# A message stream in DRAM with rows of 576 bytes in place of 516, in a two-layer graph network on one core

## What is computed

```python
h = jnp.maximum(_layernorm(x), 0.0)
# layer 0: mean over the neighbours, two products, log_softmax
agg = segment_sum(h[src], dst) / maximum(counts, 1)[:, None]
x = x + log_softmax(agg @ W_l.T + h @ W_r.T + b)
h = jnp.maximum(_layernorm(x), 0.0)
# layer 1: a weight for every edge, and a sum by the edge's source
weight = maximum(edge_attr @ W1 + b1, 0) @ W2 + b2
msg = (h @ Wl + bl)[dst] * weight
out = x + segment_sum(msg, src)
```

## Time and profile before

| | |
|---|---|
| median of 3 runs | 4677.88 us |
| the profiled execution, its own time | 4644.02 us |
| its span, first to last instruction | 4642.2 us |
| mean granted TensorE clock | 0.815 |
| busy: TensorE, VectorE, ScalarE, GpSimd | 78%, 57%, 39%, 37% |
| bytes by DMA | 468.65 MB, 101 GB/s over the span |

### The profile page before, as it was taken

One profiled execution on the slowest core, in us unless ns is written; L12 is line 12 of the kernel. 1 busy time (PEld: TensorE's weight loads), 2 busy tenths in 40 slices (PEclk: granted clock), 3 DMA queues, 4 the chain that ended last, 5 costly groups with the idle time before them and its releaser, 6 DMA issues.

```text
span 4642.2 us, 96340 instructions
## 1 busy us (share of the span) xinstructions
PE 3605.8 (78%) x24907; PEld 2626.4 (57%) x24908; DVE 2637.6 (57%) x7188; ACT 1823.9 (39%) x3754; POOL 1740.7 (37%) x1753
## 2 busy tenths in 40 slices
PE   2999999989877777777677677777777677778887
PEld 1666666657554455445455455555555445457776
DVE  7888888876444444444444444444444444457776
ACT  4666666643222222222222222222222222258887
POOL 2100000001255555555555555555555555520000
PEclk9999999995577777777777777777777777789999
DMA  3599600000023223332233333333332332258787
GB/s 90 183 318 316 212 5 6 6 1 10 23 78 76 77 76 76 78 76 77 76 76 77 76 77 76 77 77 75 78 76 77 77 76 76 76 150 223 224 225 211
DMA packets 572233, 468.65 MB, mean 101 GB/s; under 512 B 289293, under 2 KB 543334, under 8 KB 572181
## 3 DMA queue, kind: packets, MB, share of 16 engines
q1 hardware_dynamic: 515782, 348.95, 29.1%
q0 software_dynamic: 56400, 119.07, 7.5%
HBM read 235.79 MB, written 231.94 MB: 101 GB/s over the span
## 4 chain that ended last, share of the span: by engine, by line
PE 36%; another core or an unknown queue 27%; issue 18%; DVE 10%; ACT 5%; DVEq 2%; ACTq 1%; DMA 0%; POOL 0%; POOLq 0%; SPq 0%
PE PS L980 10%; PE PS L1092 5%; PE PS L1104 4%; PE PS L971 4%; DVE X L904 3%; PE PS L1081 3%; PE PS L1140 3%; DVE aux L659 2%; ACT big L1281 2%; PE PS L1073 1%; PE PS L1089 1%; ACT big L1269 1%; DVE H L893 1%; DVEq L899 1%
## 5 line engine op out<-in xcount | busy, mean ns | idle before, releaser
L492 POOL DMA_INDIRECT messages<-big,idxr x1664 | 1619.1, 973 | 1313.8 <-DVE big L865 811.4
L1104 PE MATMUL PS<-par,big 128*128 x4992 | 598.0, 268 | 753.1 <-ACT big L1281 706.7
L865 DVE TENSOR_TENSOR big<-PS,big 128x512 f32<-128x512 f32 x416 | 287.8, 692 | 1502.3 <-ACT big L1281 1142.5
L1104 PEld LDWEIGHTS PS<-par,big 128*128 128x128 bf16 x4992 | 479.6, 114 | 881.8 <-issue 805.4
L1281 ACT ACTIVATE big<-PS 128x512 f32<-128x512 f32 x416 | 248.4, 597 | 1325.3 <-remote 1121.3
L980 PE MATMUL PS<-par,aux 128*128 128x386 bf16 x3626 | 683.3, 327 | 0.0
L1092 PE MATMUL PS<-W2s,big 128*128 128x128 f32 x3328 | 678.1, 367 | 0.0
L1092 PEld LDWEIGHTS PS<-W2s,big 128*128 128x128 f32 x3328 | 576.6, 261 | 145.9 <-issue 145.9
L1202 ACT ACTIVATE aux<-PS 128x784 bf16<-128x784 f32 x592 | 479.7, 822 | 295.2 <-PE PS L971 288.2
L1269 ACT ACTIVATE big<-PS,b1c 128x512 f32<-128x512 f32 x416 | 284.4, 684 | 647.1 <-issue 424.5
L1140 PE MATMUL PS<-big,H 128*128 128x128 f32 x3456 | 444.0, 281 | 80.4 <-DVE H L893 64.1
(11 more groups left out here) (202 smaller groups left out, 3761.3 us busy)
## 6 DMA issues: line engine op xcount, KB each, us to landing
messages<-zeros SPq DMA_DIRECT2D x576, 193.5 KB
big<-messages SPq DMA_DIRECT2D x216, 516.0 KB, 3.7
aux<-slot_rows SPq DMA_DIRECT2D x416, 128.0 KB
big<-in_edge_attr_dram SPq DMA_DIRECT2D x1664, 32.0 KB
messages<-big,idxr POOLq DMA_INDIRECT x1664
X<-in_x_dram SPq DMA_DIRECT2D x6, 448.0 KB, 11.9
out_dram<-X SPq DMA_DIRECT2D x6, 448.0 KB
edge_places<-big SPq DMA_DIRECT2D x1, 2496.0 KB, 13.1
```

Of the source, the lines that this page charges most:

```text
L492: pool.indirect_dma_start(strm_d, bass.IndirectOffsetOnAxis(ap=idxr[:, n % U, j:j + 1], axis=0), outr[:, n % U, j, :], None).then_inc(S_sc ...
L1104: last = nc.tensor.matmul(pHG[:, j * C:(j + 1) * C], oht[:, k % 2, j * P:(j + 1) * P], h1p[:, ds(at + a * C, C)], start=(a == 0), stop=(a ...
```

## The change

A row of the stream gets 144 words (576 bytes) in place of 129 (516 bytes). Words 0 to 127 are the message, word 128 is the node's number, as before; the 15 words behind it are padding. The DMAs move whole rows, so the scatter, the filling with zeros and the loads of the last stage all move the padding too. The row of zeros is 2 rows long in place of 3, so the filling takes 864 DMAs of 147,456 bytes in place of 576 of 198,144. The padding in `outr` is never written by the computation, so one memset on VectorE clears the tile before the first message. ScalarE's bias takes the one column that it needs.

```diff
@@ -54,7 +54,7 @@
-    ROW = C + 1
+    ROW = C + 16
@@ -151,7 +151,7 @@
-        ZW = 3 * ROW
+        ZW = 2 * ROW
@@ -822,6 +822,7 @@
             dve.wait_ge(S["z_done"], NCH)
+            nc.vector.memset(outr, 0.0)
             nc.vector.memset(hotW, 0.0)
@@ -1302,7 +1303,7 @@
-                    last = nc.scalar.activation(away[:, t, :], iotaF[:, :], ACT.Abs, bias=fin[:, k, r, q * ROW + C:(q + 1) * ROW])
+                    last = nc.scalar.activation(away[:, t, :], iotaF[:, :], ACT.Abs, bias=fin[:, k, r, q * ROW + C:q * ROW + C + 1])
```

## The result

The changed kernel takes **4688.73 us** (median of 8 runs, 4681.45 to 4692.62), the kernel before 4678.56 in the same comparison (8 runs, 4672.25 to 4680.43). The ratio is 1.0024 [1.0015, 1.0032]: 10.2 us slower, just past the 0.2% that I said can be told. The time is 8.4 us above the forecast and inside its range. It also lies inside the 4671 to 4690 that I gave to the likeliest case, no change, but the interval of the ratio, 7 to 15 us slower, says that no change is not what came.

What follows compares the result with a forecast made beforehand. TensorE bounds layer 0, no engine is full while messages are made, VectorE's chain bounds the sums. Terms 2.4 + 0 + 0 + 0 on 4644.02 us give 4646.4; with 33.86 to the median, 4680.3 us, range 4658 to 4704.

Steps and rivals of the forecast that it cites:

- the likeliest case: Whole kernel: the forecast of 4680.3 us holds, too near the old time to tell apart, within 4671 to 4690; chance 69%.
- Zeros: Filling in layer 0: 0.55 us a DMA, 864 DMAs, done at 647 to 721 us, wanted at 1021; cost 0.
- Scatters: GpSimd's 1664 indirect DMAs while messages are made: 973 ns each as before; cost 0, with 2 us as the bound.
- The rival in which GpSimd becomes the pace: Messages: dearer scatters pace the steps, 920 us slower, or 188 us in a milder form; together 6%.
- The memset: VectorE's clearing of 2304 words ahead of the first messages: 1.9 to 2.5 us, taken as 2.4, nothing hiding it.
- a shifted rhythm: Messages: the later start shifts the pattern of steps, up to 20 us either way; 4% faster, 6% slower.
- The loads of the last stage: While messages are summed: 2.0 us on each engine, under the piece's 2.35; landings about 0.1 us later; cost 0.
- the odd piece: Last stage: an allowance of 3 us for occasional pieces delayed by a later landing, beside a cost taken as 0.
- the tight piece: Last stage: the one piece shown, ScalarE done 0.10 us before VectorE; if all 216 were so, at most 28 us; 6%.
- the sign of being wrong: Message steps shorter or longer than 6.9 us on average, or TensorE waiting for ScalarE's one-hot matrices (L1310) in the last stage.
- Faster by part-written pieces of 64 bytes: Messages: rows of 576 bytes avoid part-written pieces that hold steps back; 749 us less, a tenth being 75; 9%.
- The rule against the change: DMA reads split at 256 bytes, so whole 64-byte pieces earn nothing; a pair of rows some 4% dearer; sum unchanged.

Runs made afterwards that it cites:

- the one with the padding memset: The change with its memset on the 240 words of padding alone in place of all 2304, against the kernel before: 4652.15 us, ratio 1.0013.

## Why the prediction came out as it did

- **Zeros: right in the cost of nothing, a little dear in the size.** Forecast 0.55 us a DMA, filling done 647 to 721 us; measured 0.510 and 615, under the range. The line through 60 and 72 ns put a row of reads and a row of writes together, and the 72 has the queue's other small transfers in it; by its own working the new DMA takes 290 x 16 x 0.848 / 579 / 16 = 0.42 us on each engine for my 0.50. The cover of 300 us or more was there, and nothing moved.
- **Scatters: right.** 973 ns as before, 144 steps for 145, in traces of different clocks. The rival in which GpSimd becomes the pace did not come, nor any part of it.
- **The memset: the size right, what stood behind it left out.** 1.98 + 0.55 us for 2.4. "I take 2.4 us" was the account's whole sum for the entry. The first chip's traces put the entry at some 4 us: behind the memset TensorE does its first products at the granted clock of 0.50 where it had 1.00, and the first messages fall together in other pairs. I had named a shifted rhythm as a rival, with 6% on the slow side; the shift at the start came in every kernel with the full memset, but as a rhythm that holds on it is not shown: on the first chip the messages take as long as before. With the memset alone the median rose by 8.1 us, with an interval from 0.9 to 9.8.
- **The loads of the last stage: the step that failed.** "Landings come 0 to 0.23 us later, about 0.1 ... I take 0, and 3 us for the odd piece." I let the landing follow the engine's work, and the work was well forecast (2.05 us for 2.0). But a load lands with the last of its 16 parts, and with rows of 576 bytes the last few fall behind: 4.2 to 4.5 us in place of 3.7. I read the tight piece rightly, 0.10 us to spare; what I lacked was a landing later than my upper bound. The cost measured is 6.4 and 4.3 us in the change's two traces, and 3.0 in the one with the padding memset. What I had named as the sign of being wrong, TensorE waiting for L1310, is there with 8.0 us. That the late landings make the cost is shown from two sides: it goes with the length that lands late (572 and 580 bytes land at 3.9 and 4.0 and lose 1.0 and 1.2 us in the stage), and with eight buffers it is gone, though loads land as late. Why they land late is open.
- **Faster by part-written pieces of 64 bytes: half true and worth nothing.** The engines do have less work for the zeros of the new rows than for those of 572 bytes. The queue in 250 to 540 us, the change first and then 572 bytes:

```profile
q1 hardware_dynamic: 83280, 85.32, 84.8%
```

```profile
q1 hardware_dynamic: 79270, 80.64, 96.2%
```

290 x 16 x 0.848 / 83280 is 47.2 ns a transfer, and 290 x 16 x 0.962 / 79270 is 56.3, for zeros of 1152 and 1144 bytes (nine in ten of the queue's transfers are zeros, the rest are smaller). By the same working 1088 and 1280 bytes, whole pieces of 64 too, take 45.1 and 52.1, and 1160, which aren't, 52.5. But the 1548 bytes of the kernel before, which aren't either, take 63.9, no more a byte than the whole ones (0.041 ns). So not every transfer with a part-written piece pays alike. In the middle stage queue 1 stands at 16.5% for 19.5% in 2000 to 3000 us, with nearly the same packets. But the filling has 400 us to spare, and in the middle stage no engine waits for a DMA: the steps stayed what they were.
- **The rule against the change** (the Trainium skill, DMA: Bandwidth & Descriptors, How a descriptor splits into AXI transactions) has reads split at 256 bytes, so that whole pieces of 64 gain nothing. For reads the last stage decides nothing: 300 x 16 x 0.861 / 66518 = 62.1 ns a transfer in the change, and by the same working 62.3 at 572 bytes, no gain; but 64.1 at 580, and at 544, whole pieces again, 58.2, as little as at 516 (58.0). What it says of reads alone can't speak for the writes of the zeros, and they do gain: 47.2 for 56.3 ns. Late parts of a load follow from neither. The nearest thing in the Trainium skill (DMA: Bandwidth & Descriptors, Latency and other measured facts) is that a row pitch of large powers of two in device memory slows copies, which it puts down, as an inference, to memory channels hit in lock step; no run here reaches those pitches, and whether rows of 576 and 640 bytes meet something of the kind was not tried.
- **The sum.** Forecast +2.4, measured +10.2 and +8.4: the last stage's part is 4 to 6, the entry's some 4. Both terms erred to the same side. The range held because the odd piece and the shifted rhythm were in it; my 69% for no change leaned on a last-stage cost of zero that had a tenth of a microsecond of cover in the one piece that I read. That the time lies even inside the 69% case's 4671 to 4690 is luck: its mechanism, a last stage that loses nothing, did not hold.

## What to carry to other kernels

Where consumers take loads with little to spare, ask when the slowest of a load's 16 parts lands, not what a load costs on average: the new rows cost the engines 2.05 us a load, as forecast, and yet the loads landed later than their work says. More buffers, with the loop unrolled to match, took that cost away with its cause unknown, and paid with the old rows too (7.3 and 7.1 us). An instruction for which TensorE has to wait is to be priced with what follows it: here one of 2.5 us with its gap cost some 4, with TensorE's clock granted at the full level later behind it. And a difference of a few microseconds wants the chip on which the runs lie closest, 5.7 us against 17.9 and 18.6 here.

## What the runs showed that I had not expected

- The same kernel takes 4646.03, 4671.83 and 4675.78 us on three chips, 0.6% apart, while its 33 runs on the first span 5.7 us (4642.58 to 4648.31) and those on the others three times as much. The difference lies while messages are made: the kernel with eight buffers and rows of 516 bytes has 4103.2 - 1244.7 = 2858.5 us from first to last message on the first chip and 4131.9 - 1246.3 = 2885.6 on the third, while its last stage takes 500.6 and 501.2. The granted clock from 1270 to 4100 us is 0.73 in that trace of the first chip and 0.70 in that of the third, and 1.00 in the last stage on both.
- Zeros of 1152 bytes take 47.2 ns of an engine, of 1144 bytes 56.3, by the queue's mean.
- Loads from rows of 576 and 640 bytes land later (4.2 to 4.5 and 5.2 us) than of 572 and 580 (3.9 and 4.0), most of all in the last few of their 16 parts. Why is not shown.
- Unrolling the last stage's loop by eight in place of four gives 4.4 to 6.5 us at the same number of buffers with rows of 576 bytes (512.4 and 514.5 to 508.0), though VectorE's instructions are as long as before.
